# A two-layer graph network: counts added by VectorE and turned by a DMA, and a layer's output added to x in DRAM

## What is computed

```python
h = relu(layernorm(x))
n = ln_weight * h / rms(h)
out = n @ W_root + bias
for r in range(2):                     # mean over the edges of type r into each node
    w = (edge_type == r)
    out += segment_sum((n[src] @ W_rel[r]) * w, dst) / max(segment_sum(w, dst), 1)
x = x + h + elu(out) @ wo_weight       # end of the first layer
g = relu(layernorm(x)) @ W
e = exp(-leaky_relu(al[src] + ar[dst]))    # al, ar = g @ a_l, g @ a_r
x = x + elu(segment_sum(e * g[dst], src) / (segment_sum(e, src) + 1e-5))
```

## Time and profile before

| | |
|---|---|
| median of 3 runs | 532.58 us (531.64 to 536.67) |
| the profiled execution | 530.4 us |
| its span, first to last instruction | 528.6 us |
| TensorE busy | 502.6 us, 95% |
| VectorE busy | 368.9 us, 70% |
| ScalarE busy | 231.3 us, 44% |
| GpSimd busy | 74.6 us, 14% |
| mean granted TensorE clock | 0.994 of full speed |

### The profile page before, as it was taken

How to read it: one execution, slowest core, us unless ns; L and a number is a source line. 1 busy time by engine, 2 the same in 40 slices (tenths; PEclk the granted TensorE clock), 3 DMA queues, 4 the chain that set the end, 5 groups by cost and what they waited for, 6 DMA issues and landing times.

```text
span 528.6 us, 7977 instructions
## 1 busy us (share of the span) xinstructions
PE 502.6 (95%) x3073; PEld 433.2 (82%) x3073; DVE 368.9 (70%) x634; ACT 231.3 (44%) x386; POOL 74.6 (14%) x72
## 2 busy tenths in 40 slices
PE   3989999997899999998999999999999999999995
PEld 2889989997789999998778888888787888888885
DVE  4836885578798888855875555554798887777633
ACT  5855443407856666668733332221333322222112
POOL 1362213100000000000000000000073322222400
PEclk9999999999899999999999999999999999999998
DMA  9862273304013233225951111100022222222211
GB/s 259 223 224 79 78 236 104 118 1 110 1 50 107 81 120 115 79 79 167 311 191 39 40 39 40 39 1 0 1 78 79 78 78 79 78 79 78 79 41 41
DMA packets 22186, 49.15 MB, mean 93 GB/s; under 512 B 4798, under 2 KB 10709, under 8 KB 22018
## 3 DMA queue, kind: packets, MB, share of 16 engines
q1 hardware_dynamic: 21887, 48.33, 30.5%
q0 software_dynamic: 256, 0.26, 0.2%
HBM read 33.05 MB, written 16.85 MB: 94 GB/s over the span
## 4 chain that ended last, share of the span: by engine, by line
PE 84%; DVE 8%; ACT 5%; issue 1%; DMA 1%; SPq 0%; DVEq 0%; ACTq 0%
PE ps L1208 13%; PE ps L1433 9%; PE ps L1340 9%; PE ps L1434 9%; PE ps L1435 9%; PE ps L1414 6%; PE ps L1416 6%; PE ps L1415 6%; PE ps L1301 3%; PE ps L1363 2%; PE ps L1385 2%; PE ps L1397 1%; PE ps L1387 1%; PE ps L1386 1%; PE ps L1234 1%
## 5 line engine op out<-in xcount | busy, mean ns | idle before, releaser
L1433 PE MATMUL ps<-h_hi,att_hi 125*125 125x512 f32 (+1 forms) x190 | 73.5, 387 | 0.0
L1434 PE MATMUL ps<-h_lo,att_hi 125*125 125x512 f32 (+1 forms) x190 | 72.6, 382 | 0.0
L1435 PE MATMUL ps<-h_hi,att_lo 125*125 125x512 f32 (+1 forms) x190 | 72.5, 382 | 0.0
L1414 PE MATMUL ps<-wg,gT_hi 128*125 128x512 f32 x160 | 64.0, 400 | 0.5 <-DVE wg L1014 0.4
L1416 PE MATMUL ps<-wg,gT_lo 128*125 128x512 f32 x160 | 63.1, 394 | 0.0
L1415 PE MATMUL ps<-wg,gT_hi 128*125 128x512 f32 x160 | 63.0, 394 | 0.0
L1340 PE MATMUL ps<-msg_hi,adj_hi 125*125 125x288 f32 x200 | 56.9, 308 | 0.6 <-ACT adj_hi L579 0.5
L1340 PE MATMUL ps<-msg_lo,adj_hi 125*125 125x286 f32 x200 | 51.7, 297 | 0.0
L1208 PE MATMUL ps<-w_hi,hT_hi 128*125 128x430 f32 x128 | 46.5, 363 | 0.1
L1208 PE MATMUL ps<-w_hi,hT_lo 128*125 128x430 f32 x128 | 45.9, 358 | 0.0
L1208 PE MATMUL ps<-w_lo,hT_hi 128*125 128x430 f32 x128 | 45.7, 357 | 0.0
(11 more groups left out here) (203 smaller groups left out, 1058.8 us busy)
## 6 DMA issues: line engine op xcount, KB each, us to landing
xt<-in_x SPq DMA_DIRECT2D x10, 448.0 KB
xh_scratch<-xt SPq DMA_DIRECT2D x10, 448.0 KB
xt<-xh_scratch SPq DMA_DIRECT2D x10, 448.0 KB
x_scratch<-xt SPq DMA_DIRECT2D x10, 448.0 KB
x1t<-x_scratch SPq DMA_DIRECT2D x10, 448.0 KB
xr<-x_scratch SPq DMA_DIRECT2D x10, 448.0 KB
out_x<-xr SPq DMA_DIRECT2D x19, 224.0 KB
wg_raw<-in_L_gnn_W SPq DMA_DIRECT2D x8, 512.0 KB, 9.1
```

Of the source, the lines that this page charges most:

```text
L1414: M.matmul(to, hi, wg[k][:, 0, cut], start=n == 0, stop=False)
L1433: M.matmul(to, hi[:, s, :], h_hi[:, s, cut], start=s == 0, stop=False)
L1434: M.matmul(to, hi[:, s, :], h_lo[:, s, cut], start=False, stop=False)
L1435: return M.matmul(to, lo[:, s, :], h_hi[:, s, cut], start=False, stop=s == TILES - 1)
```

## The change

- TensorE's `counts_part` (L1363) and ScalarE's copies of them (L599) are gone from the usual path.
- VectorE gets `summed`: one addition of the two types' halves of `adj_16`, 125 x 1250 elements of 16 bits, into `sum_16` (128 x 1280, a single buffer). It has lag 2 and stands behind `one_hots(0)`. It waits until the counts of tile t are cast (`win_16`), and, from tile 1 on, until the transposing DMA of tile t - 1 has landed (`ct_out`), which reads the same buffer.
- ScalarE gets `counts_turned`: it issues a DMA that transposes `sum_16` into `counts[:, t]`. It has lag 2 and stands behind `counted(2)`. ScalarE's `counted(0)` waits for `sum_16` of tile t - 2 in place of `c_ps`.
- `output1` moves from VectorE to ScalarE (lag 2, at the end of the step), where it is a copy from PSUM to `xt`. GpSimd then issues two DMAs for each tile (`output_added`) that add `xt` to `xh_dram`, waits for them, and only then counts up `x1_done`; ScalarE's `output1` of tile t waits for `x1_done` of tile t - 2.
- SP no longer reads `xh_dram` back (`load_xh`) or stores `x1_dram` (`store_x1`); `load_x1` and `load_xr` read `xh_dram`. The last two loads of `wg` wait for the last `ct_out` in place of `c_ps`.
- Two copies of the identity matrix to other types are gone from the usual path.
- The branch for edges that are not found (`If_ne`), which does not run on this data, is changed to fit, and is cut here.

```diff
-            def load_xh(t, b):
-                if t < 2:
-                    sp.wait_ge(S["xh_out"][b], came_x(TILES - 2 + b, b))
-                else:
-                    if t < AHEAD:
-                        sp.wait_ge(S["xh_ahead"][b], 32)
-                    sp.wait_ge(S["x1_out"][b], came(t - 2, b))
-                move(xt[b], row(xh_dram, t), ("xb_in", b))
-
-            def store_x1(t, b):
-                sp.wait_ge(S["x1_rdy"], data(t))
-                move(row(x1_dram, t), xt[b], ("x1_out", b))
...
-            for t in range(TILES):
-                if t == 4:
-                    load_x1(0, 0)
-                    load_x1(1, 1)
-                if t == TILES - 2:
-                    sp.wait_ge(S["rows_free"], 1)
-                    for k in ORDER[0:2]:
-                        load_wg(k)
-                    load_x1(2, 0)
-                    sp.wait_ge(S["s_ps"], data(TILES - 1))
-                    for k in ORDER[2:6]:
-                        load_wg(k)
-                    sp.wait_ge(S["c_ps"], 3 * data(TILES - 1))
-                    for k in ORDER[6:8]:
-                        load_wg(k)
-                    for first, end in ((0, BAND), (BAND, T)):
-                        sp.dma_start(a_b[first:end], a_gat.rearrange("o (s d) -> (o s) d", s=2).partition_broadcast(end - first)).then_inc(S["a_in"], 16)
-                if t == TILES - 1:
-                    load_x1(3, 1)
-                store_x1(t, t % 2)
-                if t + 2 < TILES:
-                    load_xh(t + 2, t % 2)
+            load_x1(0, 0)
+            load_x1(1, 1)
+            sp.wait_ge(S["rows_free"], 1)
+            for k in ORDER[0:2]:
+                load_wg(k)
+            load_x1(2, 0)
+            sp.wait_ge(S["s_ps"], data(TILES - 1))
+            for k in ORDER[2:6]:
+                load_wg(k)
+            sp.wait_ge(S["ct_out"], 16 * TILES)
+            for k in ORDER[6:8]:
+                load_wg(k)
+            for first, end in ((0, BAND), (BAND, T)):
+                sp.dma_start(a_b[first:end], a_gat.rearrange("o (s d) -> (o s) d", s=2).partition_broadcast(end - first)).then_inc(S["a_in"], 16)
+            load_x1(3, 1)
             for t in range(4, TILES):
...
+            def output_added(t, b, d):
+                pool.wait_ge(S["x1_rdy"], data(t))
+                for first, end in ((0, BAND), (BAND, T)):
+                    G.dma_start(row(xh_dram, t)[first:end], xt[b][first:end], accum_op=ALU.add).then_inc(S["x1_out"][b], 16)
+                pool.wait_ge(S["x1_out"][b], came(t, b))
+                pool.sem_inc(S["x1_done"], 1)
+            pool.sem_inc(S["x1_done"], CREDIT)
+            for b in range(2):
+                pool.wait_ge(S["xh_ahead"][b], 32)
+                pool.wait_ge(S["xh_out"][b], came_x(TILES - 2 + b, b))
+            pipeline((output_added, 0))
...
-                    act.wait_ge(S["c_ps"], 3 * room(t))
+                    if usual:
+                        act.wait_ge(S["sum_16"], room(t))
+                    else:
+                        act.wait_ge(S["c_ps"], 3 * room(t))
...
+            def counts_turned(t, b, d):
+                act.wait_ge(S["sum_16"], data(t))
+                act.dma_start(counts[:, t], sum_16[:].rearrange("p n s -> p (n s)"), transpose=True).then_inc(S["ct_out"], 16)
...
+            def output1(t, b, d):
+                act.wait_ge(S["o_ps"], data(t))
+                act.wait_ge(S["x1_done"], room(t))
+                A.copy(xt[b][:].rearrange("p (h n) -> p h n", h=2), ps[0:T, 6:8, :]).then_inc(S["x1_rdy"], 1)
+
+            def output1_placed():
+                act.sem_inc(S["x1_rdy"], CREDIT)
+                for b in range(2):
+                    act.wait_ge(S["xh_out"][b], came_x(TILES - 2 + b, b))
...
-                pipeline((counted(0), 0), (y_split, 2), (counted(1), 0), (counts_part(0), 1), (counted(2), 0), (elu, 1), (counts_part(1), 1),
-                         (counted(3), 0), (counts_part(2), 1), (counted(4), 0), opening=split_wo, before=2, steps=(0, TILES))
+                pipeline((counted(0), 0), (y_split, 2), (counted(1), 0), (counted(2), 0), (counts_turned, 2), (elu, 1),
+                         (counted(3), 0), (counted(4), 0), (output1, 2), opening=split_wo, before=2, steps=(0, TILES))
+                counts_turned(TILES - 2, 0, 4)
                 act.sem_inc(S["rows_free"], 1)
                 last, before = (TILES - 1, 1, 4), (TILES - 2, 0, 4)
                 y_split(*before)
                 deviation2(0, 0)
                 deviation2(1, 1)
                 norm2(0, 0)
-                counts_part(0)(*last)
                 norm2(1, 1)
+                counts_turned(*last)
+                back_to_exp()
+                elu(*last)
+                output1(*before)
                 transposed2(0, 0, 0)
-                back_to_exp()
-                counts_part(1)(*last)
-                elu(*last)
-                counts_part(2)(*last)
                 y_split(*last)
                 split_gat_weights(range(0, 2))
+                output1(*last)
                 transposed2(1, 1, 0)
                 second_layer()
...
+            def summed(t, b, d):
+                mine = slice(T * b, T * (b + 1))
+                dve.wait_ge(S["win_16"], done(nth(t, NG - 1)))
+                if t == 0:
+                    V.memset(sum_16[:], 0).then_inc(S["pad_rdy"], 1)
+                    dve.wait_ge(S["pad_rdy"], 1)
+                else:
+                    dve.wait_ge(S["ct_out"], 16 * t)
+                V.tensor_tensor(sum_16[0:T, :, 0:T], adj_16[:, 0:TILES, mine], adj_16[:, TILES:BLOCKS, mine], ALU.add).then_inc(S["sum_16"], 1)
...
-            def output1(t, b, d):
-
-                dve.wait_ge(S["o_ps"], data(t))
-                dve.wait_ge(S["xb_in"][b], came(t, b))
-                V.tensor_tensor(xt[b][:].rearrange("p (h n) -> p h n", h=2), ps[0:T, 6:8, :],
-                                xt[b][:].rearrange("p (h n) -> p h n", h=2), ALU.add).then_inc(S["x1_rdy"], 1)
...
-                pipeline((one_hots(0), 0), (one_hots(1), 0), (y_split, 3), (one_hots(2), 0), (z_of, 2), (one_hots(3), 0), (y_of, 2),
-                         (one_hots(4), 0), (lambda t, b, d: split_wo() if t == 0 else None, 2), (output1, 3), steps=(0, TILES))
+                pipeline((one_hots(0), 0), (summed, 2), (one_hots(1), 0), (y_split, 3), (one_hots(2), 0), (z_of, 2), (one_hots(3), 0), (y_of, 2),
+                         (one_hots(4), 0), (lambda t, b, d: split_wo() if t == 0 else None, 2), steps=(0, TILES))
+                summed(TILES - 2, 0, 4)
                 y_split(TILES - 3, 1, 3)
                 last, before = (TILES - 1, 1, 4), (TILES - 2, 0, 4)
                 z_of(*before)
                 variance2(0, 0)
                 y_of(*before)
                 variance2(1, 1)
-                output1(TILES - 3, 1, 3)
                 y_split(*before)
                 deviation2(0, 0)
                 deviation2(1, 1)
-                transposed2(0, 0, 0)
+                summed(*last)
                 z_of(*last)
                 y_of(*last)
-                output1(*before)
+                transposed2(0, 0, 0)
                 y_split(*last)
                 split_gat_weights(range(0, 2))
                 variance2(2, 0)
-                output1(*last)
                 second_layer()
...
+            def y_transposed(t, b, d, usual=False):
                 pe.wait_ge(S["y_rdy"], data(t))
-                pe.wait_ge(S["c_used"], 3 * t + 2 + 3 * CREDIT)
+                if usual:
+                    pe.wait_ge(S["yT_lo_rdy"], room1(t))
+                else:
+                    pe.wait_ge(S["c_used"], 3 * t + 2 + 3 * CREDIT)
...
-                pipeline((counted(0), 0), (y_transposed, 2), (summed(0), 1), (counted(1), 0), (summed(1), 1), (counts_part(0), 1), (counted(2), 0),
-                         (output1(0), 2), (counts_part(1), 1), (counted(3), 0), (output1(1), 2), (counts_part(2), 1), (counted(4), 0), steps=(0, TILES))
+                turned = lambda t, b, d: y_transposed(t, b, d, True)
+                pipeline((counted(0), 0), (turned, 2), (summed(0), 1), (counted(1), 0), (summed(1), 1), (counted(2), 0),
+                         (output1(0), 2), (counted(3), 0), (output1(1), 2), (counted(4), 0), steps=(0, TILES))
                 last, before = (TILES - 1, 1, 4), (TILES - 2, 0, 4)
-                y_transposed(*before)
-                counts_part(0)(*last)
+                turned(*before)
                 summed(0)(*last)
-                transposed2(0, 0, 0)
                 summed(1)(*last)
-                counts_part(1)(*last)
                 output1(0)(*before)
                 output1(1)(*before)
-                counts_part(2)(*last)
-                y_transposed(*last)
+                transposed2(0, 0, 0)
+                turned(*last)
                 transposed2(1, 1, 0)
                 output1(0)(*last)
                 output1(1)(*last)
...
```

(30 more changed lines are left out.)

41 lines of the change are left out of this document (18 added, 23 removed).

## The result

| | before | after |
|---|---|---|
| median (lowest to highest), us | 533.24 (531.64 to 536.67) | 602.9 (602.14 to 605.38) |
| ratio to before, 95% interval | | 1.1344 (1.1304 to 1.1384) |
| profiled execution, its span, us | 530.4, 528.6 | 603.0, 601.2 |

The change costs 70 us. The forecast was 604 us with a range of 570 to 632, and its mechanism, the ring of waits, is what the profile shows. That it came within about 1 us is luck: its term for the DMA was too large by 1.9 us a step, and two slow DMAs and a longer tail, which it put at nothing, made up for it.

The account below looks back on a forecast made before the run. TensorE's order of work was taken as the bound. A step of 11.6 + 3.8 + 5.4 + 1.7 = 22.5 us gave +6.8 (first tile) + 68.6 (seven steps) - 1.3 = +74 on 530.4, so 604 us, range 570 to 632.

Parts of the forecast that it names:

- the ring of waits: Stage 2, each step: output1(0) waits for y_split, behind summed, behind a DMA issued after counted(2); 3.8 us plus the DMA.
- Rival 1: Stage 2: no ring, or the DMA has landed when VectorE asks; TensorE stays the bound, 518 us; chance 0.05.
- What TensorE gives back: TensorE, stage 2: without L1363's 1.15 us, 11.55 us of work remain in a 12.70 us step, taken as 11.6.
- The DMA, D = 5.4: Transposing DMA of the counts, issue to landing: 5.4 us, the middle between 2.9 and 7.7.
- rival 3: Transposing DMA is dear, as every element is written by itself: D = 15 us, 681 us in all; chance 0.10.
- From counted(2) to output1(0), the rest: Each step's wait without the DMA: ScalarE's eviction 0.84 us, then VectorE's summed, one_hots(1) and y_split; 3.8 us together.
- The clock, 1.7 a step: TensorE behind each idle gap: half speed for 3.6 us, losing 1.7 us a step; 0 kept as possible.
- The tail, 0: From output1(0) of tile 7 to the end: 0 put, nothing to differ by over 3 us.
- Rival 5: GpSimd's adding DMAs set the pace, ScalarE's copy waiting for x1_done; at 25 us a tile 624 us; chance 0.04.
- rival 2: Ring there but cheap: D = 2.9 and full clock, 570 us; the forecast's low end, within its 0.75.
- rival 4: TensorE's clock stays at 1.2 GHz through whole steps of stage 2: +61, so 665 us; chance 0.04.
- rival 6: Total within 1% of before, the ring open in most steps and the few others eating the gain; chance 0.02.

Follow-up runs that it names:

- p_lag1: Against plain, ScalarE's counts_turned at lag 1 in place of 2, so each tile's DMA is issued one step earlier: 528.12 us.
- p_counts_lag1: As p_lag1, but only the counts part of the change, with the output added by VectorE and stored by SP as before: 525.53 us.
- plain: The changed kernel with a plain DMA of the same 128 x 1280 values for the transposing one, transposition left out: 597.58 us.
- p_filled: Against plain, TensorE does 42 idle products ahead of seven of the eight waits of output1(0): 585.75 us.
- p_counts_table: Against p_counts_lag1, ScalarE's wait for the last counts DMA moved to behind the attention's table load: 523.36 us.
- p_lag1_tail: Against p_lag1, all eight wg loads ahead of tile 2's x rows, and ScalarE's wait for the counts moved behind the table load: 531.32 us.
- p_lag1_mid: Against p_lag1, six wg loads in place of two ahead of tile 2's x rows, and ScalarE's counts wait behind the table load: 526.31 us.
- output_alone: The kernel before with only the output part: ScalarE copies out, GpSimd's DMAs add in DRAM, counts as before: 533.91 us, ratio 1.003.

## Why the prediction held, and where it did not

- **The ring.** Right in place, count and releasers: eight waits of TensorE ahead of output1(0), released by y_split, with the DMA behind them. p_lag1 shows the cause: one step of lag is worth 69.5 us. Rival 1's condition, with the DMA issued a step before it is asked for, gave 528.12, where the rival had 518: of its seven steps p_lag1 has the full 7.7 us, but tile 0 starts 1.1 us later than in before, and the last stages take 4.3 us back.
- **What TensorE gives back.** 11.6 us a step was right (11.6 in p_lag1 and p_counts_lag1).
- **The DMA, D = 5.4.** Mis-sized. It was 3.5, near the low bound of 2.9. The middle between bounds far apart (5.3 exactly, not 5.4) was taken because a transpose "scatters 2-byte elements over partitions", and rival 3 had "every element is written by itself". Against the plain DMA the transposition made only 0.9 us of difference, and the page of after counts 13120 packets for the 3.28 MB of the ten DMAs, 250 bytes each (plain: 1440 packets). The Trainium skill ("DMA: Bandwidth & Descriptors", Latency and other measured facts, and its anatomy of one DMA, which describes one issued by GpSimd) had led to an estimate of 3.3 us, and the trace agrees within 0.2. What neither had is the landing of 6.1 to 6.3 us beside the x1t loads, twice.
- **From counted(2) to output1(0), the rest.** 3.8 us was taken, 0.65 + 2.9 = 3.5 measured. The DMA does issue beside the cast and not behind it, and the addition takes 0.73 us.
- **The clock, 1.7 a step.** Right in kind and nearly in size: 20.6 - 7.03 - 11.6 = 2.0 us in after. In plain the same sum gives 20.45 - 6.05 - 11.6 = 2.8, of which the products of p_filled gave 2.3 back.
- **The step, 22.5.** 11.6 + 3.5 + 3.5 + 2.0 = 20.6 us. The seven steps gave +60.2 in place of +67.3; the two slow DMAs put 5 to 6 of it back. Tile 0 was +5.7, forecast +6.8.
- **The tail, 0.** The step of the prediction that failed: "From output1(0) of tile 7 to the end nothing differs by over 3 us" was 6.7. I had looked for work and not for the orders of SP and ScalarE. SP's timeline of after:

```profile
318.49 0.77 SPq L279 DMA_DIRECT2D x1t<-xh_scratch  x2
319.31 3.58 SPq L341 DMA_DIRECT2D wg_raw<-in_L_gnn_W  x6
```

  The x rows of tile 2 wait for room that TensorE's transposed2(0) gives, which the change moved behind output1 of tile 8; six of the weight loads stand behind them. They are issued 319.31 - 301.25 = 18.1 us behind output1(0) of tile 7, where before had 14.0 (249.42, SP's timeline). TensorE waits for wg at 330.51 (2.37 us) and 339.72 (0.59), where before had 0.38 in all, and its clock is 0.50 from 330.2 to 333.6 us, which costs another 1.5. The table load behind the new wait adds 1.3 us of gap ahead of the attention, and from the attention's first product to the end after takes 148.8 us against 147.7, with the clock at 0.50 from 453.1 to 456.5. In p_counts_table moving that wait took back 2.2 in the median and 1.4 in the span, from p_counts_lag1, whose clock was full behind the gap.

  How the wait for wg divides between SP's order and the adding DMAs of tile 8, which GpSimd issues at 319.52 right beside these loads, no run shows alone: p_lag1_tail and p_lag1_mid change the order and move the wait without removing it, and p_counts_lag1, which has no adding DMAs, waits 1.55 us with p_lag1's distance of 15.8 us.
- **The adding DMAs and the rest of output1.** Rival 5 fell: ScalarE's copy waited 3.5 us in all, for TensorE. They cost nothing in stage 2 (output_alone, +0.3% in all). That they may slow the loads of wg behind it was in no term and no rival.
- **Rivals 2, 3, 4, 6.** D was near rival 2's 2.9, but the full clock that it also needs was not there: 570 was out of reach. 3, 4 and 6 fell with D = 3.5, with the clock full again 4 us behind each gap, and with the ring in every step.

With 3.5 for D, 3.5 for the rest, 2.0 for the clock, and 5.7 for tile 0, the sum would have been 5.7 + 7 x (20.6 - 12.7) - 1.3 = 59.7, or 590 us; the two slow DMAs (5 to 6) and the tail (6.7) make it 602. The forecast met 603 because 1.9 us too much for D in each of eight waits, some 15 us, stood in place of these.

## What to carry to other kernels

A DMA in a hand-written order is cheap or dear by its lag: with the same plain DMA, which landed in 2.6 us, the kernel was 66 us over before when the consumer stood in the same turn as the issue, and 4 us under it when it stood a turn later. Draw the ring of waits through all queues for each new wait, and count the clock behind every gap of TensorE as part of its price. When an instruction is moved or a queue gets a wait ahead of it, look at what that queue issues next (weights, a table load), and check first that the engine relieved is the one that sets the pace.

## What the runs showed of the hardware

- A transposing DMA of 128 x 1280 values of 2 bytes, on-chip to on-chip, landed in 3.5 us and took ScalarE's queue 1.35 us to issue; a plain one of the same bytes 2.6 and 0.47.
- Beside 500 KB loads of x1t the same DMAs took up to 6.3 us (transposing) and 5.4 us (plain); in p_counts_lag1 and p_counts_table the plain one beside them took 7.3 and 7.9 us.
- Around gaps of 7.0 us (after) and of 6.05 us (plain) the granted clock was 0.50 for the same 6.8 us. It fell 4.0 to 4.4 us into the longer gaps and 4.9 to 5.0 us into the shorter ones, so that TensorE worked some 4 and 5.7 us at it: a shorter wait was not a shorter low clock. What sets the point at which it falls was not settled.
- GpSimd's adding DMAs of 448 and 52 KB landed in 4.9 us at the median, about 1.5 times the 3.2 us of a plain store and its wait.
- Six loads of 512 KB issued together landed in 8.6 to 14.8 us with GpSimd's adding DMAs just ahead of them (p_lag1), and in 6.5 to 11.5 us without them (p_counts_lag1).
